# Turned probabilities of heads 0 and 1 of each quarter: into the score banks instead of the PSUM ring

## The reference, cut to what matters

```
x = x + 0.5 * ffn(layernorm(x))        # pass 1
x = x + attn(layernorm(x))             # linear attention, between the passes
x = x + 0.5 * ffn(layernorm(x))        # pass 2

def ffn(x):                            # 16 heads of 64, 8 experts, 2 chosen
    q, k = x @ Wq[h], x @ Wk[h]
    v = sum over 2 chosen experts of sigmoid(gate) * (x @ Wv[e])
    probs = softmax(q * 64**-0.5 @ k.T)     # 256 x 256 per head
    attn = probs @ v
    return sum over 2 chosen experts of attn @ Wo[e]
```

## Time and profile before

| | |
|---|---|
| median of three runs | 2620.91 us (2619.99 to 2627.41) |
| the profiled execution's own time | 2622.49 us |
| its span | 2620.7 us |
| TensorE matmuls busy | 98% of the span |
| TensorE weight loads busy | 88% |
| VectorE busy | 75% |
| ScalarE busy | 72% |
| GpSimd busy | 35% |
| granted TensorE clock, mean | 0.997 |

### The profile page before, as it was taken

The page is one execution under the profiler, slowest core; times in us unless marked ns, Lnnn a source line. Parts: engine busy times, 40 slices in busy tenths (PEclk is TensorE's granted clock), DMA queues, the critical chain, the costliest instruction groups (busy, mean ns, idle before and its releaser), DMA issues.

```text
span 2620.7 us, 106485 instructions
## 1 busy us (share of the span) xinstructions
PE 2564.3 (98%) x43776; PEld 2311.8 (88%) x43776; DVE 1970.5 (75%) x3434; ACT 1886.4 (72%) x5989; POOL 915.4 (35%) x806
## 2 busy tenths in 40 slices
PE   5999999999999999999999999999999999999998
PEld 4899998999989889898889899898999988998987
DVE  6777777777777777777777777777777777777774
ACT  3777777777777777776777777777777777777775
POOL 2243443433423423424334233333243342333321
PEclk9999999999999999999999999999999999999999
DMA  4655555565565555555555655655555555555553
GB/s 132 164 140 149 145 137 151 142 157 153 146 156 148 142 156 150 150 153 143 154 151 146 157 146 143 158 143 157 151 145 155 152 143 151 144 147 151 149 151 105
DMA packets 519326, 387.26 MB, mean 148 GB/s; under 512 B 214080, under 2 KB 436160, under 8 KB 510656
## 3 DMA queue, kind: packets, MB, share of 16 engines
q1 hardware_dynamic: 518416, 379.60, 54.1%
q10 hardware_dynamic: 432, 0.85, 0.1%
HBM read 191.64 MB, written 188.74 MB: 145 GB/s over the span
## 4 chain that ended last, share of the span: by engine, by line
PE 88%; ACT 5%; DVE 4%; issue 2%; DMA 0%; POOL 0%; ACTq 0%; DVEq 0%; POOLq 0%; SPq 0%
PE psS L385 18%; PE psT L427 17%; PE psT L465 17%; PE psT L444 7%; PE psT L445 5%; PE psT L446 5%; PE psT L439 4%; PE psT L397 4%; PE psT L411 4%; ACT PB L785 3%; DVE NMAX L686 2%; ACT VM L793 1%; PE psT L506 1%; DVE XT L662 1%; PE psT L558 1%
## 5 line engine op out<-in xcount | busy, mean ns | idle before, releaser
L785 ACT ACTIVATE PB<-psS,NMAX 128x256 f32<-128x256 f32 x2048 | 943.5, 488 | 554.4 <-DVE NMAX L686 554.4
L686 DVE TENSOR_REDUCE NMAX<-psS 128x4 f32<-128x1024 f32 x512 | 602.7, 1219 | 86.3 <-PE psS L385 86.3
L427 PE MATMUL psT<-V,PT 128*64 128x64 f32 x16384 | 540.6, 224 | 8.4 <-issue 7.9
L427 PEld LDWEIGHTS psT<-V,PT 128*64 128x64 f32 x16384 | 503.0, 138 | 49.3 <-issue 32.8
L898 POOL TENSOR_TENSOR BT<-MT,diagv 128x1024 f32<-128x1024 f32 x128 | 306.2, 2392 | 652.9 <-DMA MT<-MIXd 652.9
L465 PE MATMUL psT<-ident,PB 128*128 128x128 f32 x4096 | 515.8, 277 | 8.8 <-ACT QK L823 2.8
L766 DVE COPY PT<-psT 128x512 f32<-128x512 f32 x512 | 348.0, 689 | 220.6 <-PE psT L465 219.9
L385 PE MATMUL psS<-QK 64*128 64x256 f32 x4096 | 512.7, 390 | 0.0
L465 PEld LDWEIGHTS psT<-ident,PB 128*128 128x128 f32 x4096 | 448.2, 142 | 53.2 <-ACT QK L823 17.0
L785 ACT ACTIVATION_READ_ACCUMULATOR PB<-psS,NMAX 128x1 f32 x2048 | 452.4, 221 | 0.0
L385 PEld LDWEIGHTS psS<-QK 64*128 64x128 f32 x4096 | 375.5, 187 | 77.3 <-issue 33.6
(11 more groups left out here) (115 smaller groups left out, 4137.3 us busy)
## 6 DMA issues: line engine op xcount, KB each, us to landing
Vd<-VM SPq DMA_DIRECT2D x128, 512.0 KB, 3.7
V<-Vd SPq DMA_DIRECT2D x128, 512.0 KB, 5.3
AOd<-AO SPq DMA_DIRECT2D x256, 256.0 KB, 3.5
PJd<-PJ SPq DMA_DIRECT2D x64, 512.0 KB, 2.6
PR<-PJd SPq DMA_DIRECT2D x64, 512.0 KB, 4.1
MIXd<-MIX SPq DMA_DIRECT2D x64, 128.0 KB, 2.5
MT<-MIXd SPq DMA_DIRECT2D x64, 128.0 KB, 5.1
MASKd<-MASKR SPq DMA_DIRECT2D x64, 128.0 KB, 2.4
```

The lines of the kernel that those rows point to most:

```text
L427: last = eng.matmul(M[64 * u:64 * u + 64, (t * NT + it) * DH:(t * NT + it + 1) * DH], PT[:, t, jt, cols], V[:, pm % 2, 4 * r + t, jt, :], ...
L686: eng.tensor_reduce(NMAX[:, ab, :, :], psS[:, ab, :, :, :], AX_X, ALU.max, negate=True).then_inc(s_max)
L785: eng.activation(PB[:, ab, j, it, :], psS[:, ab, j, it, :], ACT.Exp, bias=NMAX[:, ab, j, it:it + 1], accum_out=SUM[:, p % 2, it, head:head ...
```

## The change

Turnings 0 and 1 of a quarter leave the ring and are written into `psS[:, 0, 0]` and `psS[:, 0, 1]`, the banks in which the scores of the same two heads lay. By then their exponentials have been taken. They get semaphores of their own: `s_turned` counts turnings, `s_copied[0]` and `s_copied[1]` count ScalarE's copies of turning 0 and VectorE's of turning 1. The scores of pair 0 (`ab == 0`) of the next quarter wait for both copies. The waits of turnings 0 and 1 for a vacant bank are gone, and the ring holds two items less in each quarter, so what lies four places before an item is another item than it was. Order of the work, operations and sizes stay. The diff, cut to its core:

```diff
             if works(n):
-                items += [("turn", n, t) for t in range(4)]
+                items += [("turn", n, t) for t in (2, 3)]
...
+        def turned(n, t):
+            return psS[:, 0, t].rearrange("p n t -> p (n t)") if t < 2 else bank("turn", n, t)
+        def wait_turned(eng, n, t):
+            if t < 2:
+                eng.wait_ge(s_turned, 2 * n + t + 1)
+            else:
+                wait_full(eng, "turn", n, t)
+        def was_turned(n, t):
+            return s_turned if t < 2 else full("turn", n, t)
+        def was_copied(n, t):
+            return s_copied[t] if t < 2 else freed("turn", n, t)
+        def wait_copied(eng, n, t):
+            if t < 2:
+                eng.wait_ge(s_copied[t], n + 1)
+            else:
+                wait_freed(eng, "turn", n, t)
...
                 if n >= 1:
                     eng.wait_ge(s_exp, 8 * (n - 1) + 4 * ab + 4)
+                if n >= 1 and ab == 0:
+                    wait_copied(eng, n - 1, 0)
+                    wait_copied(eng, n - 1, 1)
...
                 for t in range(4):
-                    wait_freed(eng, "turn", m, t)
+                    wait_copied(eng, m, t)
...
             def turn(n, t):
                 ab, j = divmod(t, 2)
-                wait_vacant(eng, "turn", n, t)
+                if t >= 2:
+                    wait_vacant(eng, "turn", n, t)
                 eng.wait_ge(s_exp, 8 * n + 2 * t + 2)
-                M = bank("turn", n, t)
+                M = turned(n, t)
...
-                last.then_inc(full("turn", n, t))
+                last.then_inc(was_turned(n, t))
...
-                        wait_full(eng, "turn", n, t)
+                        wait_turned(eng, n, t)
                         wait_full(eng, "product", n - 1)
-                        eng.tensor_copy(PT[:, t].rearrange("p n t -> p (n t)"), bank("turn", n, t)).then_inc(freed("turn", n, t))
+                        eng.tensor_copy(PT[:, t].rearrange("p n t -> p (n t)"), turned(n, t)).then_inc(was_copied(n, t))
```

More of the change, by code:

```diff
@@ L217, in macaron_kernel @@
         s_free = [semaphore(f"s_free{i}") for i in range(BANKS)]
+        s_turned = semaphore("s_turned")
+        s_copied = [semaphore(f"s_copied{i}") for i in range(2)]
         s_value = [semaphore(f"s_value{i}") for i in range(2)]
@@ L778, in exponentials @@
                 eng.wait_ge(s_max, 2 * n + ab + 1)
-                wait_full(eng, "turn", n - 1, 2 * ab + 1)
+                if n >= 1:
+                    wait_turned(eng, n - 1, 2 * ab + 1)
                 if r == 0 and ab == 0 and p >= 2:
@@ L877, in scalar_program @@
                     for t in (0, 2):
-                        wait_full(eng, "turn", n, t)
+                        wait_turned(eng, n, t)
                         wait_full(eng, "product", n - 1)
-                        eng.activation(PT[:, t].rearrange("p n t -> p (n t)"), bank("turn", n, t), ACT.Copy).then_inc(freed("turn", n, t))
+                        eng.activation(PT[:, t].rearrange("p n t -> p (n t)"), turned(n, t), ACT.Copy).then_inc(was_copied(n, t))
         @block.gpsimd
```

## The result

The change makes the kernel slower: 2644.77 us (median of six runs, 2643.29 to 2647.04) against 2622.14 us for the kernel before beside it, a ratio of 1.0083 with a 95% interval of 1.007 to 1.0096. That is 22.6 us more; the forecast was 15 us more, on 2620.9. The profiled execution has a span of 2643.0 us against 2620.7, 22.3 us more.

What follows compares the result with a forecast made beforehand. TensorE was taken as the bound, with 88% of the chain. Losses 24.1 and 10.2 less gains 10.9, 7.3 and 4.7 gave +11.4 us; with 4 us for jitter the forecast was +15, 2636 us, range 2616 to 2652.

Steps and rivals of the forecast that it cites:

- The ring's relief: TensorE's weight loads before the transposes: 19.8 us idle for q and k, 10.3 us for x's remainder, nearly all recoverable.
- loss 1: 28 quarters with r = 0: scores wait for VectorE's late copy of turning 1, 0.86 us each, 24.1 us.
- Loss 2: 29 quarters with r = 2 without the attention's x: scores wait for VectorE's copy, 0.35 us each, 10.2 us.
- Gain 1: r = 2 with the attention's x: turning 1 no longer waits for the turned x's bank, 0.33 us, 33 times, -10.9 us.
- gain 2: r = 0 with the attention's output product: transposes no longer wait for ring banks, 0.28 us in 26 quarters, -7.3 us.
- Gain 3: r = 3 with the attention's turning: 0.18 us less within the turnings in 26 quarters, -4.7 us.
- the handover: From a VectorE result to the weight load it releases: 0.06 us, with waits met in time taken as 0.
- 4 us for all: Unmeasured cost of releases met with 0.01 us to spare before the scores: 0.02 us for copy jitter, 4 us in all.
- (a): Faster: changed timing moves GpSimd's spread off VectorE's work before the copy at r = 0; -9 us, 2612 us, 12%.
- (c): Much slower: scores' loads refill after each release, 0.16 us in some 200 quarters; +43 us, 2664 us, 8%.
- (b): No measurable change: no jitter, VectorE late by 0.1 us less in each of 57 quarters; +6 us, 2627 us, 27%.
- (d): Pair 0's turnings held by ScalarE's exponentials, not the ring, so no gain appears; +38 us, 2659 us, 3%.

Runs made afterwards that it cites:

- 1: Kernel before with only the new rule: pair 0's scores also wait for the copies of turnings 0 and 1, which stay in the ring; 2668.99 us, ratio 1.0183.
- 2: Changed kernel with the pairs exchanged: turnings 2 and 3 come first, into pair 1's banks, turnings 0 and 1 use the ring; 2578.88 us, ratio 0.9839.
- experiment 8: Changed kernel with GpSimd's spread of the gates cut to the first eighth of each half, the rest zeroed once at the start; 2619.68 us, ratio 0.9996.
- Experiment 4: Changed kernel with the four waits before the scores turned round: VectorE's copy, ScalarE's, q and k, exponentials in the source; 2620.83 us, ratio 1.0001.
- both repairs: Waits turned round and VectorE's choice step behind its copies: in the changed kernel 2601.03 us, ratio 0.9935; with the pairs exchanged 2574.58 us, ratio 0.9829.
- 3: Changed kernel with one semaphore for both copies, so one wait in place of two before the scores; 2640.32 us, ratio 1.0079.
- 5: Changed kernel with only the wait for the exponentials moved behind the two copies' waits in the source; 2660.8 us, ratio 1.0152.
- 9: Kernel before with only the new waits added, put ahead of the others in the source, last in the compiled program; 2649.3 us, ratio 1.0115.
- 12: Kernel before with the turnings in the order 2, 3, 0, 1, all four in the ring; 2620.57 us, ratio 1.0007.

## Why the prediction was right, and where its terms were off

**Direction, range and mechanism.** Slower, inside the range (2616 to 2652), with 2644.8 against 2636. The ring's relief and the copies' wait are the two sides of the sum, as the kernels with the wait alone (1) and with the relief nearly alone (2) show. That the forecast came within 8 us is in part luck: 9 us of handover that the sum did not have were hidden by 9 us by which other stretches got shorter, and loss 1 came near its figure because its errors offset each other (below).

**The terms.** For each set of quarters I compared the two profiles, from one scores group to the next. Loss 1: 22.4 us (24.1 forecast), and experiment 8 shows its cause. But the copy came 0.26 us sooner after the first transpose than in the kernel before (1.87 against 2.13 on average), while the transposes came 0.11 later and the scores 0.10 later after the copy's end than forecast: the three nearly cancel. Loss 2: 11.8 (10.2); the 0.35 a quarter was 0.44, by the dearer release. Gain 1: 9.1 (10.9), gain 2: 5.6 (7.3); both smaller by the same 0.07 to 0.09 a quarter. Gain 3: a loss of 1.0 (gain of 4.7). The sum of these is 20.6 us, against 11.4.

**The step that was mis-sized** is the handover: "From a VectorE result to the weight load that it releases I take 0.06 us", and with it "waits that are met in time cost nothing, and I take 0". The 0.06 came from a load that carries the late wait itself. Ahead of the scores two or three met waits stand behind the late one, and the load takes 0.115 or 0.225. In the 114 quarters in none of the sets this gives 0.07 to 0.08 each, 9 us over the stretch from transpose to scores, where the prediction had 4 us for all. The row that I used for the waits, five ahead of the output product, shows only waits that were all met while TensorE was still at work: it says nothing of a wait behind a late one. Experiment 4, where none stands behind VectorE's, has 0.053 in the late quarters and 1.84 in the plain ones: the prediction's handover.

**Gain 3** had a second error. Half of the merged row of 1.18 us was taken for one copy of 0.6, but the two copies in that row overlap, and the first takes 0.69 us. It also starts at the same place in the quarter before and after (8.88 and 8.87 us after the first scores), so what the transposes gain by starting 0.23 earlier can't reach the scores. With 0.69 and the handover of experiment 4 this set gains 2.8 us, with that of the changed kernel it loses 1.0.

**What happened against the sum.** The 114 other quarters also got 9 us shorter in the stretch from scores to transposes. All of it lies in 14 of them, which are 0.2 to 1.7 us shorter than before; the typical one is unchanged. Two of the 14 lie at the start and the end (3 us), most of the others had irregular stops in the kernel before (below). No term of the prediction stands for this, and it hides the 9 us of the handover there. The start took 1.3 us longer.

**The rivals.** (a) The spread did move off the state's arithmetic (L768 at 281 ns), but in 15 of the 28 quarters it held L604 in its place, in 8 still L768, and the copy was nearly as late: the place of the blow changed more than its size. The prediction looked at one victim and should have looked at the whole queue ahead of the copy. The kernel before shows as much: L740 was held in 21 of the 28, L576 (L604 after) in 5, and in the two quarters of the earlier trace rows it was L580, at 2.60 and 2.48 us:

```profile
126.92 2.60 DVE L580 TENSOR_TENSOR FW<-EQ,rampb 128x512 bf16<-128x512 bf16 x1
...
2498.89 2.48 DVE L580 TENSOR_TENSOR FW<-EQ,rampb 128x512 bf16<-128x512 bf16 x1
```

(c) The refill after each release, priced at 0.16 a quarter, was the right kind of term at half its size, for another reason. (b) and (d) did not come.

## What to carry to other kernels

When a buffer is reused by its own successor, count the time from the last reader to the next writer at every turn, on every engine in between; here the same relief was worth a loss of 22 us with the pair that is needed first and a gain of 42 us with the pair that is needed 0.8 us later; with both repairs it is a gain of 18 us against one of 45. Put the wait that comes last in time where the compiled program passes it last, on the instruction that needs it, and read that order from the compiled program, not from the source: in these kernels the wait written first in the source stood on the load. Price a handover from a row in which as many waits stand behind the late one as in your case.

## What the runs showed of the hardware that was not expected

**Met waits behind a late one.** To the matmul one cost 0.05 us, two 0.09, three 0.20 (experiments 3 to 5, confirmed by 9). What is shown is the place of the late wait: on the load, on the semaphore instruction ahead of it, or on the one before that. Whether a met wait costs by itself, or only the instruction that carries it, isn't separated: no run has a late wait alone on the instruction next to the load.

**Who is held by GpSimd.** VectorE instructions with both operands in SBUF were stretched while GpSimd's spread of 2.4 us ran: L740 from 0.28 to between 1.2 and 2.3 us in 21 of 32 places, L580 from 0.41 to 2.60, L604 (after) from 0.69 to as much as 2.88. With a short spread L740's 32 places are all short (experiment 8). The Trainium skill (SBUF — State Buffer, Who interferes with whom) has this as a lock on a shared port that the first instruction holds whole. The trace agrees, and shows beyond it that moving the spread moves the victim to another two-operand instruction of VectorE.

**Irregular stops.** Between quarters 8 and 247 the kernel before has 22 stretches from scores to transposes that are more than 0.15 us over the median of their kind, 9 us in sum, and the kernel after 8 with 4 us, in other places. One of them (quarter 115) is a stop of 0.43 us between two matmuls of `product` whose loads have no wait on them; the profile calls it "issue". The four kernels with all turnings in the ring (before, 1, 9, 12) have 12 to 22 such quarters, the other ten 1 to 15, so the change may bear on them; what they are was not tried.
